# Bias loads on ScalarE's DMA queue, weight maxima in landing order, and the residuals of the value and output weights inside head 0

## What is computed

```python
xn = _layernorm(x)
q = (xn @ Wq + bq).reshape(b, h, t, dh)          # k, v alike
logits = jnp.einsum('bhtd,bhds->bhts', q, k) * scale
weights = jax.nn.softmax(logits + mask, axis=-1)
out = jnp.einsum('bhts,bhsd->bhtd', weights, v)
attn = out.transpose(0, 2, 1, 3).reshape(b, t, h * dh) @ Wo + bo
return x + attn + moe(xn)   # top-6 of 64 experts, capacity 128, and a shared expert
```

## Time and profile before

| | |
|---|---|
| median of 3 runs | 1937.94 us (1934.93 to 1942.94) |
| profiled execution | 1938.18 us |
| its span | 1936.4 us |
| instructions | 49605 |
| busy: PE, DVE, POOL, ACT | 86%, 80%, 60%, 56% of the span |

### The profile page before, as it was taken

One profiled execution on the slowest core, in us unless ns is written; L12 is line 12 of the kernel. 1 busy time (PEld: TensorE's weight loads), 2 busy tenths in 40 slices (PEclk: granted clock), 3 DMA queues, 4 the chain that ended last, 5 costly groups with the idle time before them and its releaser, 6 DMA issues. The chain is left out here.

```text
span 1936.4 us, 49605 instructions
## 1 busy us (share of the span) xinstructions
PE 1670.1 (86%) x19088; PEld 1298.5 (67%) x19088; DVE 1539.5 (80%) x3187; ACT 1087.6 (56%) x2348; POOL 1157.8 (60%) x1005
## 2 busy tenths in 40 slices
PE   1499989999899999999877789989998999989996
PEld 1376766777677777777756667766676776667674
DVE  4888878888888888888854448988988898988885
ACT  0466556666566666666542236565665555566564
POOL 1146657777677777777660026666766666666653
PEclk9799999999999999999996779999999999999998
DMA  9455656565755556555557738777878787777864
GB/s 312 165 95 116 120 115 122 121 113 102 123 91 95 96 93 101 93 92 92 114 91 208 215 82 140 124 131 132 145 127 143 123 143 135 131 123 127 151 116 100
DMA packets 692691, 245.03 MB, mean 127 GB/s; under 512 B 643552, under 2 KB 680753, under 8 KB 691568
## 3 DMA queue, kind: packets, MB, share of 16 engines
q1 hardware_dynamic: 665584, 199.92, 56.0%
q0 software_dynamic: 18432, 33.64, 7.1%
q10 hardware_dynamic: 8448, 8.39, 1.3%
HBM read 57.11 MB, written 50.46 MB: 56 GB/s over the span
## 5 line engine op out<-in xcount | busy, mean ns | idle before, releaser
L479 POOL TENSOR_TENSOR prob<-prob 128x128 f16<-128x128 f32 (+7 forms) x512 | 659.9, 1292 | 619.5 <-ACT prob L855 613.2
L848 ACT ACTIVATE prob<-prob,nmax 128x128 f32<-128x128 f32 (+7 forms) x512 | 397.0, 775 | 648.1 <-DVE prob L1271 637.8
L690 PE MATMUL ps_s<-kT,qT 128*128 128x512 f16 (+3 forms) x2304 | 458.2, 326 | 9.8 <-DVE kT L1258 6.2
L705 PE MATMUL ps_o<-probT,vh 128*128 128x256 f16 (+1 forms) x3840 | 426.2, 264 | 3.9 <-DMA probT<-prob 3.9
L1271 DVE TENSOR_SCALAR_CACHE_REDUCE prob<-ps_s,neg_scale 128x128 f32<-128x128 f32 (+7 forms) x512 | 409.7, 808 | 3.3 <-PE ps_s L692 2.6
L705 PEld LDWEIGHTS ps_o<-probT,vh 128*128 128x128 f16 x3840 | 368.0, 99 | 48.1 <-issue 4.4
L855 ACT CAST prob<-prob 128x128 f16<-128x128 f32 (+7 forms) x512 | 341.4, 667 | 2.3
L690 PEld LDWEIGHTS ps_s<-kT,qT 128*128 128x128 f16 x2304 | 199.9, 98 | 149.4 <-issue 12.1
L719 PE MATMUL ps_y<-wo,oT 128*128 128x256 f16 x1536 | 211.3, 274 | 86.0 <-DVE oT L1286 68.7
L582 PE MATMUL ps_t<-xT,wq 128*128 128x64 f16 x6144 | 201.4, 195 | 60.5 <-DVE z L1173 23.6
L582 PEld LDWEIGHTS ps_t<-xT,wq 128*128 128x128 f16 x6144 | 192.4, 99 | 72.2 <-issue 29.8
(11 more groups left out here) (173 smaller groups left out, 1821.1 us busy)
## 6 DMA issues: line engine op xcount, KB each, us to landing
dispatched<-zeros SPq DMA_DIRECT2D x16, 512.0 KB, 14.6
probT<-prob SPq DMA_TRANSPOSE x512
ex<-dispatched SPq DMA_DIRECT2D x16, 512.0 KB, 4.3
expert_out<-eo ACTq DMA_DIRECT2D x16, 512.0 KB, 3.9
eup<-in_L_ffn_w_up_dram SPq DMA_DIRECT2D x64, 64.0 KB, 2.1
resid<-in_L_attn_x_dram SPq DMA_DIRECT2D x1, 3072.0 KB, 11.8
dispatched<-xn,slot_idx POOLq DMA_INDIRECT x192
xn_columns<-xnth SPq DMA_DIRECT2D x24, 128.0 KB
```

Of the source, the lines that this page charges most:

```text
L479: pool.tensor_tensor(low_cols(j), prob_cols(j).rearrange("p (r k) -> p r k", k=P), high_cols(j), ALU.subtract).then_inc(p_low, 1)
L690: pe.matmul(s_cols(j, lo, hi), qT[:, u, a, j * P:(j + 1) * P], kT[:, u, c, lo:hi], start=(n == 0), stop=(n == 2 and hi < w))
L705: mm = pe.matmul(ps_o[:, lo:2 * P], vh[:, u, a, r * D:(r + 1) * D], probT[:, PT_AT[c] + 2 * r + s, lo:], start=(r + n == 0), stop=(r == 2 ...
L848: nc.scalar.activation(prob_cols(j), prob_cols(j), ACT.Exp, bias=nmax[:, j:j + 1], scale=-1.0, accum_out=rsum[:, i % 2, j:j + 1]).then_inc ...
```

## The change

Parts of it:
- bq, bk, bv are loaded from ScalarE's queue, as its first instructions, with a semaphore of their own (`bias_in`). VectorE waits for these three; `w_in` (five DMAs) is waited for only ahead of the constant row.
- SP loads Wo ahead of Wv. Wo is staged in the place of batches 2 and 3 of `resid`; those are loaded by ScalarE's queue in head 1. The other staging buffers move, and the small scale tiles now lie in a region that is reused later. Since Wv's buffer lies under `probT`, SP's first transpose waits for `wsplit[2]`.
- VectorE takes the maximum of Wq before the low half of x transposed, and the maximum of Wo before that of Wv.
- The second round of scales, and the high and low parts of Wv and Wo, move into head 0. VectorE writes Wo's low part from the unscaled buffer; ScalarE's in-place scaling and GpSimd's subtraction are gone.

```diff
 @block.sync
-            for n in range(2):
-                sp.dma_start(stg[n][:].rearrange("p (k n) -> p k n", k=KC), views[n]).then_inc(wload[n], 16)
-            sp.dma_start(bqT[:], bq.rearrange("(m d) -> d m", d=D)).then_inc(w_in, 16)
-            sp.dma_start(bkT[:], bk.rearrange("(m d) -> d m", d=D)).then_inc(w_in, 16)
-            for n in range(2, 4):
...
-            sp.dma_start(bvT[:], bv.rearrange("(m d) -> d m", d=D)).then_inc(w_in, 16)
+            for n in (0, 1, 3, 2):
+                sp.dma_start(stg[n].rearrange("p (k n) -> p k n", k=(KC, KC, KC, H)[n]), views[n]).then_inc(wload[n], 16)
...
-            sp.dma_start(resid[:, TB:, :], x_v[:, TB:, :]).then_inc(x_in[1], 16)
+            sp.dma_start(resid[:, TB:2 * TB, :], x_v[:, TB:2 * TB, :]).then_inc(x_in[1], 16)
...
             def transpose_probs(i, j):
+                if i + j == 0:
+                    sp.wait_ge(wsplit[2], 1)
 @block.gpsimd
-            pool.wait_ge(whigh, 5)
-            pool.tensor_tensor(wo[:, 1, :, :].rearrange("p a b -> p (a b)"), stg[3][:],
-                               wo[:, 0, :, :].rearrange("p a b -> p (a b)"), ALU.subtract).then_inc(wsplit[3], 1)
 @block.scalar
+            act.dma_start(bqT[:], bq.rearrange("(m d) -> d m", d=D)).then_inc(bias_in, 16)
+            act.dma_start(bkT[:], bk.rearrange("(m d) -> d m", d=D)).then_inc(bias_in, 16)
+            act.dma_start(bvT[:], bv.rearrange("(m d) -> d m", d=D)).then_inc(bias_in, 16)
             act.wait_ge(var_ready, 1)
...
-            for n in range(4):
-                w, scale = (wq, wk, wv, wo)[n], scales[:, n:n + 1]
-                act.wait_ge(wscale_step, 8 * (n // 2) + 8)
...
-            act.wait_ge(cvec_done, 1)
-            nc.scalar.activation(stg[3][:], stg[3][:], ACT.Copy, scale=scales[:, 3:4]).then_inc(whigh, 1)
+            def high_weights(n):
+                act.wait_ge(wscale_step, 8 if n < 2 else 21)
...
+            high_weights(0)
+            high_weights(1)
...
                     softmax_exp(i, 0)
+                    if i == 0:
+                        high_weights(2)
+                    if i == 1:
+                        act.wait_ge(wsplit[3], 1)
+                        act.wait_ge(cvec_done, 1)
+                        for b in range(2, B):
+                            act.dma_start(resid[:, b * TB:(b + 1) * TB, :], x_v[:, b * TB:(b + 1) * TB, :]).then_inc(x_in[2], 16)
...
                     softmax_exp(i, 2)
+                    if i == 0:
+                        high_weights(3)
 @block.vector
-            dve.wait_ge(w_in, W_IN)
...
             weight_max(0)
-            weight_max(1)
-            weight_bounds(0)
...
             for n in range(4):
                 k, part = n % 2, n // 2
                 dve.wait_ge(xt0_high, n + 1)
...
+            dve.wait_ge(bias_in, 48)
+            V.tensor_copy(bvB[:], bvT[:].unsqueeze(2).to_broadcast([P, H, P])).then_inc(bias_ready, 1)
+            V.tensor_reduce(biasmax[:, 0:1], bqT[:], AX.X, ALU.max, apply_absolute_value=True).then_inc(wmax_step, 1)
+            V.tensor_reduce(biasmax[:, 1:2], bkT[:], AX.X, ALU.max, apply_absolute_value=True).then_inc(wmax_step, 1)
+            weight_max(1)
+            weight_bounds(0)
+            weight_scales(0)
+            bank_scales(0)
+            weight_max(3)
+            low_weights(0)
             weight_max(2)
-            low_weights(0)
+            weight_bounds(1)
             low_weights(1)
...
+            total_constant()
...
                 elif i == 2:
+                    dve.wait_ge(x_in[2], 32)
...
                 low_k(i0, 0)
+                if i0 == 0:
+                    weight_scales(1)
+                    bank_scales(1)
...
                     if odd >= 0:
                         shared_hidden(odd, 1)
+                    if i == 0:
+                        low_weights(2)
...
                         shared_hidden(odd, 2)
+                    if i == 0:
+                        low_weights(3)
                     block_max(i, 4)
```

More of the change, by code:

```diff
@@ L104, in causal_attention_with_moe, with psb @@
         bvB = pro.enter_context(nc.sbuf_tensor("bvB", [P, H, P], F32))
+        def psb(name, shape, dt=F32):
+            return pro.enter_context(nc.sbuf_tensor(name, shape, dt))
+        bvT = psb("bvT", [P, H])
+        absmax = psb("absmax", [P, 4])
+        biasmax = psb("biasmax", [P, 2])
+        bound = psb("bound", [P, 4])
+        bounds = psb("bounds", [P, 4])
+        expo_u = psb("expo_u", [P, 4], U32)
+        expo = psb("expo", [P, 4])
+        sinv_u = psb("sinv_u", [P, 4], U32)
+        scale_u = psb("scale_u", [P, 4], U32)
         pro.close()
@@ L140, in causal_attention_with_moe @@
         ps_y = ctx.enter_context(nc.psum_tensor("ps_y", [P, 512], F32))
-        x_in = [sem(f"x_in{n}") for n in range(2)]
+        x_in = [sem(f"x_in{n}") for n in range(3)]
+        bias_in = sem("bias_in")
         w_in = sem("w_in")
@@ L252, in causal_attention_with_moe @@
         pro = ExitStack()
[L254 to L267, removed]
+        stg = [pro.enter_context(nc.sbuf_tensor(f"stg{n}", [P, KC * HD], F32)) for n in (2, 1, 0)][::-1]
+        xn0 = pro.enter_context(nc.sbuf_tensor("xn0", [P, TB, C], F32))
         pro.close()
+        stg = [t[:] for t in stg] + [resid[:, 2 * TB:, :].rearrange("p t c -> p (t c)")]
         tmp = ExitStack()
@@ L287, in causal_attention_with_moe @@
         eo = sb("eo", [P, 2, EG, C])
-        W_IN = 16 * 8
+        W_IN = 16 * 5
         S_BANK = (0, 1, 2, 3, 0, 2, 0, 2)
@@ L838, in _ @@
                 nc.scalar.copy(xT[:, 0, k, part * 512:(part + 1) * 512], ps_s[:, n // 2, n % 2 * 512:(n % 2 + 1) * 512]).then_inc(xt0_high, 1)
-            for n in range(4):
-                w, scale = (wq, wk, wv, wo)[n], scales[:, n:n + 1]
-                act.wait_ge(wscale_step, 8 * (n // 2) + 8)
-                nc.scalar.activation(w[:, 0, :, :].rearrange("p a b -> p (a b)"), stg[n][:], ACT.Copy, scale=scale).then_inc(whigh, 1)
-            act.wait_ge(cvec_done, 1)
-            nc.scalar.activation(stg[3][:], stg[3][:], ACT.Copy, scale=scales[:, 3:4]).then_inc(whigh, 1)
+            def high_weights(n):
+                act.wait_ge(wscale_step, 8 if n < 2 else 21)
+                nc.scalar.activation((wq, wk, wv, wo)[n][:, 0, :, :].rearrange("p a b -> p (a b)"), stg[n],
+                                     ACT.Copy, scale=scales[:, n:n + 1]).then_inc(whigh, 1)
+            high_weights(0)
+            high_weights(1)
             def softmax_exp(i, j):
@@ L1107, in low_weights, with bank_scales, total_constant @@
             def low_weights(n):
-                w = (wq, wk, wv)[n]
+                w = (wq, wk, wv, wo)[n]
                 dve.wait_ge(whigh, n + 1)
-                V.scalar_tensor_tensor(w[:, 1, :, :].rearrange("p a b -> p (a b)"), stg[n][:], scales[:, n:n + 1],
+                V.scalar_tensor_tensor(w[:, 1, :, :].rearrange("p a b -> p (a b)"), stg[n], scales[:, n:n + 1],
                                        w[:, 0, :, :].rearrange("p a b -> p (a b)"), ALU.mult, ALU.subtract).then_inc(wsplit[n], 1)
-            dve.wait_ge(w_in, W_IN)
-            V.tensor_reduce(biasmax[:, 0:1], bqT[:], AX.X, ALU.max, apply_absolute_value=True).then_inc(wmax_step, 1)
-            V.tensor_reduce(biasmax[:, 1:2], bkT[:], AX.X, ALU.max, apply_absolute_value=True).then_inc(wmax_step, 1)
+            def bank_scales(r):
+                two = slice(2 * r, 2 * r + 2)
+                inv = scale_u[:].bitcast(F32)
+                wstep(V.tensor_scalar(scale_u[:, two], sinv_u[:, two], 23, None, ALU.logical_shift_left))
+                if r == 0:
+                    wstep(V.tensor_tensor(logit_scale[:], inv[:, 0:1], inv[:, 1:2], ALU.mult))
+                    wstep(V.tensor_scalar(neg_scale[:], logit_scale[:], -SCALE, None, ALU.mult))
+                    wstep(V.tensor_scalar(bqT[:], bqT[:], scales[:, 0:1], None, ALU.mult))
+                    wstep(V.tensor_scalar(bkT[:], bkT[:], scales[:, 1:2], None, ALU.mult))
+                else:
+                    wstep(V.tensor_tensor(out_scale[:], inv[:, 2:3], inv[:, 3:4], ALU.mult))
+                    wstep(V.tensor_scalar(out_scale[:], out_scale[:], 1.0 / O_SHIFT, None, ALU.mult))
+            def total_constant():
+                dve.wait_ge(w_in, W_IN)
+                dve.wait_ge(cvec_done, 1)
+                V.tensor_tensor(cvec[:], ps_y[:, 0:C], cvec[:], ALU.add).then_inc(cvec_ready, 1)
             weight_max(0)
-            weight_max(1)
-            weight_bounds(0)
-            V.tensor_copy(bvB[:], bvT[:].unsqueeze(2).to_broadcast([P, H, P])).then_inc(bias_ready, 1)
-            weight_scales(0)
             for n in range(4):
@@ L1149, in later_stats @@
                     dve.wait_ge(x_in[1], 16)
+                elif i == 2:
+                    dve.wait_ge(x_in[2], 32)
                 if i < 6:
```

17 lines of the change are left out of this document (1 added, 16 removed).

## The result

Over 20 runs of each kernel the changed one takes 1933.06 us in the median (1928.67 to 1937.14), the one before 1937.61 (1932.55 to 1942.94). The ratio is 0.9978 with a 95% interval of 0.9969 to 0.9987: 4.3 us faster by the ratio (the medians are 4.55 apart), a third of the 12.7 that were forecast. The profiled execution took 1928.67 us, span 1926.9. The times of both kernels scatter by 8 to 10 us, so one pair of profiles can't give the total; the first 110 us repeat far better (in a second profile of each kernel T0 and the start of head 1 moved by 0.2 to 0.6 us) and are read here.

What follows compares the result with a forecast made beforehand. VectorE alone was taken to set the time of the first 110 us. Gains of 20.1 and 5.1 less losses of 11 and 1.5 gave 12.7 us, so 1925.3 us, range 1916 to 1937.

Steps and rivals of the forecast that it cites:

- T0: Start of head 0's first bias addition on VectorE: forecast at 58.0 us instead of 78.14, 20.1 us gained.
- tb: Landing of the last of three bias loads in ScalarE's queue: forecast 29.7 us; region 25 to 35 had chance 0.45.
- one for one: Rival on DMA queue sharing: one small packet passes per large one, tb 39.6 us, kernel 1935 us; chance 0.15.
- The row at 1404.7 us: Trace of 0.9 us where 99 small packets passed beside 62 large gather packets; the forecast took 1.6 per large one from it.
- ScalarE's hold: ScalarE's square root waits behind three bias issues, to about 18.5 us; costed at nothing in the forecast.
- From tb to T0: VectorE's list of weight maxima, scale steps and residuals after the bias wait: forecast sum 28.3 us.
- T0 to the first block: Stretch to head 0's first row maximum: forecast 7.7 us instead of 12.8, 5.1 us gained, as GpSimd's residual is gone.
- Head 0: Wv's and Wo's residuals moved in, V projection late and perhaps at half clock: 11 us lost, within 9.5 to 12.3.
- Head 1: Reload of x for the last two batches takes DMA time from transposes: 1.5 us lost, within 0 to 6.
- Later heads: Head 2 and later were forecast to run as before, carrying the gain at head 1 to the end.

Runs made afterwards that it cites:

- e5: The changed kernel with the three bias loads issued behind ScalarE's square root and four copies of x transposed: 1948.1 us, ratio 1.0047 to the kernel before.
- e4: The kernel before with only Wo's low part moved from GpSimd to VectorE, from the unscaled buffer, ahead of head 0: 1933.3 us, ratio 0.9972.
- e7: e6 with the second round of scales and Wv's and Wo's high and low parts back ahead of head 0: 1913.1 us, ratio 0.9876 to the kernel before.
- e2: The kernel before with only the bias loads moved first into ScalarE's queue, with their own semaphore, other small loads awaited at the constant row: 1941.3 us, ratio 1.0011.
- e3: The kernel before with bias loads in SP's queue directly behind x, their own semaphore, other small loads awaited at the constant row: 1917.4 us, ratio 0.9896.
- e1: The changed kernel with the three bias loads back in SP's queue, behind the first load of x and ahead of Wq: 1913.6 us, ratio 0.9877 to the kernel before.
- e6: The changed kernel with biases loaded in contiguous 512-byte rows, still first in ScalarE's queue, and transposed by TensorE: 1910.4 us, ratio 0.9856 to the kernel before.
- e8: e6 with Wv's residual moved ahead of the row maxima of blocks 2 and 3 in head 0: 1913.7 us, ratio 0.9875 to the kernel before.

## Why the prediction was wrong, point by point

**The step that failed is tb.** It put 29.7 us, by 1.6 small packets for each large one, and the runs show one for one and 42.9, outside the 25 to 35 that the prediction had set as its own bounds. The row at 1404.7 us was rightly chosen and wrongly used: its 99 beside 62 is a count over all 16 DMA engines and 0.9 us. Cut finer, the same trace says more. From 1404.70 to 1405.12 us, with the gather at 84.9% of the engines' time:

```profile
q0 software_dynamic: 15, 0.06, 84.9%
q1 hardware_dynamic: 17, 0.00, 6.8%
```

From 1405.14 to 1405.24 us 62 passed beside 23, and the rest of the 0.9 us, those 17 beside 15 included, has 37 beside 39. So the whole surplus comes from 0.1 us, and the rest is near one for one, though smaller cuts of it scatter (12 beside 4 from 1404.86 to 1405.16 us). That it ran on engines where no gather packet stood is a reading; the view doesn't tell the engines apart. A ratio from a mixed window is an upper bound for how well small packets fare. The rival "one for one" named that reading and gave it 0.15. It should have had the forecast's place: one for one is the only ratio that the row allows if single packets take turns, which the text had itself concluded. The rival's own landing of 39.6 was 3.3 us short. Up to 42.9 us q10 has 6192 packets and 10.8% of the engines' time, which is 4.6 us for each engine where I had 2.9; and q1 has 6605, which is 413 for each engine where I had 384. So its 1935 lies near the measured 1933.1 in part by luck: with the true landing it would be 1938.5, and other terms and the later heads took off 5 us.

The Trainium skill (DMA: Bandwidth & Descriptors, Queues, rings and completion order) has the turns right: a DMA engine goes round its queues packet by packet. Its typical packets of 9 to 17 descriptors aren't what these queues did: the profile counts each element as a packet, and one element passed for one row.

**ScalarE's hold.** Predicted to about 18.5 us, rows at 23, line 1125 done at 30, at no cost. Measured 20.0, 25.3, 32.0. The table load of 1.28 us, which used to run during x's load, now stands behind the issues; I had not counted it. At no cost is right: VectorE was done at 32.0 and stood still until 42.9, and in e5, without the hold, T0 still follows the last bias by 27.2 us.

**From tb to T0.** 28.3 us summed, 27.2 measured (42.93 to 70.17). The step from the bound to the first scale is 0.7 us, not 1.6: GpSimd's maximum over partitions took 0.37 us here against 1.24 before. Its times go with what VectorE runs over it, which no run tested by itself: the copy of bv lay over it before, nothing did in the first round of the changed kernel, and in its second round, where the residual of Wk lies over it, it took 4.50 us. The rest agrees within 0.2.

**T0 to the first block.** 7.7 predicted, 7.5 measured. That the 8.03 us were GpSimd's doing was read from the overlap of two rows; e4 shows it. The Trainium skill's rule (SBUF — State Buffer, Practical consequences), that a VectorE instruction with two SBUF inputs contends with a GpSimd instruction that reads SBUF, is borne out: in head 0 GpSimd's low part of block 3 takes 5.01 us where it took 1.16, under VectorE's residual of Wo. SP's transpose of that block waits for it and starts at 99.37, as it ends; as predicted, no computing engine waited.

**Head 0.** The loss was put at 11 us within 9.5 to 12.3; head 0 takes 29.5 us instead of 19.1, so 10.4 (30.1 and 18.8 in the second profiles, so 11.3). The V projection ran partly cold, as feared. The table of stretches of the changed kernel (granted clock in the third column from the end) while TensorE waits for the residual, and when V begins:

```profile
84.00:88.00 4.00, 0.00 (x0) 0.00 (x0) 4.00 (x1) 4.00 (x3) 0.04 (x1) 0.55 0.00 0
88.00:90.00 2.00, 1.60 (x16) 1.61 (x17) 0.94 (x2) 1.25 (x4) 1.10 (x1) 0.50 0.14 30
```

The clock fell to 0.50 in the gap, and V's 48 matmuls took 4.19 us instead of 2.84.

**Head 1.** 1.5 us were put down for the reload of x; head 1 takes 27.81 instead of 26.56: 1.25. The reload shows in SP's queue: a transpose issued at 112.58 us holds SP for 7.16 us, where the same one took 3.10 before, and TensorE then waits 1.94 us for a transposed tile at 123.08, where before it waited for none. In e7, which also has the reload, these are 6.03 and 1.09 us, and head 1 takes 26.97; why it costs less there is open.

**Sum at head 2.** With the measured tb and my other terms the sum is a loss of 0.5 us; the profiles have a gain of 1.5 and 0.4. The terms behind tb were good to 2 us together.

**Later heads.** "Head 2 and later should run as before" was wrong by about 3 us, and part of the 4.3 seems to lie there. I compared the distances between the starts of heads in ten profiles, five of kernels with the prologue of before (before, its second profile, e2, e3, e4), five with that of the change (after, its second profile, e1, e5, e6). Up to head 33 the two groups have the same mean from head 3 on (816.2 and 816.4 us). From head 34 to head 63 the first group takes 743.9 to 745.7, the second 740.9 to 743.5. Head 49 takes 27.4 to 27.5 us in four of the first group (25.86 in e4) and 25.86 to 25.88 in all of the second; head 47 differs by 0.2 to 0.9. The loss in head 49 goes with the granted clock. The table of stretches of the kernel before, and of the changed one at the same place in the head:

```profile
1534.00:1536.00 2.00, 2.00 (x12) 1.49 (x11) 2.00 (x5) 1.01 (x3) 1.58 (x2) 0.55 1.12 235
```

```profile
1528.00:1530.00 2.00, 2.00 (x21) 1.77 (x20) 2.00 (x4) 0.76 (x3) 1.78 (x3) 1.00 1.12 227
```

TensorE had waited 2.0 us for VectorE just ahead of the first and 1.65 us ahead of the second. The one was followed by a clock of 0.55, the other by 1.00. e4 has no such dip in head 49, but head 36 takes 27.46 us there against 25.8 to 25.9 in all others. So such dips come and go between kernels that are the same from head 3 on. e7 and e8, which stand outside the two groups, have no dip in head 49 (25.87 and 25.86 us) and take 741.5 and 741.2 us from head 34 to 63. Why the changed kernel has fewer is open.

**The range and the chances.** 1933.1 us lies inside 1916 to 1937. The effect is a third of the forecast one: the point was too early by the 13 us of tb, less 2 us of other terms and some 3 us in the later heads.

## What to carry to other kernels

Before a load is put in a second DMA queue, count its packets per DMA engine, not its bytes: 24 KB in 6144 packets landed only when the queue beside them had moved 14.4 MB, in about as many packets, and was well into the zero fill. Load such a vector in contiguous rows and transpose it on chip, or put it in the first queue ahead of the bulk, where T0 came 1.4 us later than with rows (50.20 in e1, 48.84 in e6). A ratio read from a mixed window is a bound: cut the window finer, and price the strictest reading first. And when a short VectorE instruction takes ten times its usual time, look for a GpSimd instruction over it before counting the wait to something else.

## What the runs showed of the hardware

- Two hardware DMA queues with work took strict turns by packet, 214 beside 214 with 8 KB rows and 567 beside 569 with 1 KB rows, in the changed kernel. e5 found the same later, in the zero fill: 881 beside 881 from 42 to 50 us.
- A DMA issue can hold its engine: 7.94 and 10.66 us on ScalarE for the second and third load of 2048 elements, 12.68 on SP before, 13.87 on SP in the changed kernel for Wv, the fifth load of its queue, and 0.43 to 0.45 for each of e6's three. I read it as a full queue; no run shows how much a queue holds.
- A VectorE instruction with two SBUF inputs was held 7.3 us by a GpSimd subtraction, and GpSimd 3.9 us by a VectorE residual.
- After a gap of TensorE of 6.2 us in head 0 the granted clock was 0.50; after one of 2.0 us in head 49 it was 0.55, after one of 1.65 us it stayed at 1.00.
